# A reordering of the attention stages' queues in a macaron transformer block on one core

## The chip, the core and the metric

The kernel runs on one core of one Trainium2 chip. The metric is the device time of one execution in microseconds. All engines run side by side: TensorE (PE in the profile), VectorE (DVE), ScalarE (ACT), GpSimd (POOL) and the DMA queues of SyncE (SP); each executes its own list of instructions in the order in which it is written, and waits on semaphores that the others raise.

## The reference

The input x has 2 batches of 2048 rows of 256 numbers. Three blocks are added to it in turn, each of them reading a layer-normalised x:

```
x = x + 0.5 * ffn(layernorm(x))
x = x + attention(layernorm(x))
x = x + 0.5 * ffn(layernorm(x))

ffn:        gate = fp4(x) @ fp4(w_gate).T ; up = fp4(x) @ fp4(w_up).T
            h = silu(gate) * up           ; out = fp4(h) @ fp4(w_down).T
attention:  q, k, v = x @ W.T + b   (real and imaginary parts, 256 each)
            scores = (qr.kr + qi.ki) / 16 ; w = softmax(scores)
            out = stack(w @ vr, w @ vi) @ Wo + bo
```

`fp4` quantises blocks of 16 numbers to the FP4 grid and back. Everything is float32.

## The kernel before, in words

**Split numbers.** To keep float32 accuracy, a value that goes into TensorE is held as two float32r parts, the upper (`_hi`) and the lower (`_lo`), and a product is three matmuls.

**Attention.** The weights of queries and keys are multiplied together once, and so are those of values and output, so that attention has one key tensor `k`, one query tensor and one value tensor of width 256. The work goes in 8 stages, `n = 0 .. 7` (`NQ = 8`), each of 512 rows of queries; stages 0 to 3 belong to batch 0, stages 4 to 7 to batch 1 (`HQ = 4`). A stage walks over 16 chunks `c` of 128 keys (`CH = 16`). In this text S(n,c) is `scores(n, c)`, six matmuls of 512 columns, and W(n,c) is `weighted_values(n, c)`, twelve matmuls of 256 or 258 columns. For a chunk:

1. PE makes S(n,c) in one of two PSUM banks; `scores` waits until the copy out and the running maximum of chunk c-2 are done (`evac_done`, `top_done`).
2. ACT copies the scores to a ring in SBUF (`evacuate`, L1453); DVE keeps the running maximum (`running_top`, L913), which waits for that copy.
3. After the stage's last chunk, PE transposes the maximum, DVE reduces it and makes the shift, PE spreads the shift over a bank.
4. DVE subtracts the shift (`shifted`, L935), ACT takes the exponential (`exponential`, L1459) and writes the upper part (`p_upper`, L1469), POOL writes the lower part (`p_lower`, L553).
5. PE makes W(n,c), which waits for `p_lower`, and accumulates it in four banks. At the end of a stage DVE divides by the row sum and adds to x (`finish`, L939 and L945), after W(n,15).

Steps 4 and 5 of stage n-1 run beside steps 1 and 2 of stage n: on PE, S(n,c) and W(n-1,c') alternate. In most stages W(n-1,c-2) follows S(n,c). W(n-2,15) comes behind S(n,0). W(n-1,0) also waits for `finish(n-2)`. `p_upper(n,c)` waits for W(n,c-4), as there are four buffers of upper parts.

**Where the lists differ by stage.** At n = 3 and n = 7 `SCORES_ALONE` names chunks at which a score runs with no W behind it. At n = 1 and n = 5 the last two value tiles are made just ahead of the stage (`values_upper`, L1443, on ACT and `values_lower`, L898, on DVE). At n = 4 the batch changes: PE transposes the keys of batch 1 in groups (`transpose_keys(1, g)`, L1606, called TK1, TK2 and TK3 here for g = 1 to 3), ACT writes their upper part (`keys_upper`, L1244), DVE their lower part (`keys_lower`, L884), and `queries(4)` (L1908) is made from group 0. TK1 writes the banks in which the queries of stage 4 stand, so it waits until ACT's `queries_upper` (L1435) and DVE's `queries_lower` (L890) have read them (`qlo_done`). Its input `xn` is written by DVE or POOL (`keys_normalised`, L983 on DVE). TK2 waits for the lower part of group 1, TK3 for that of group 2, and S(4,0) for that of group 3.

**After attention.** The second FFN's first steps are laced into the last stage's W by an order written out by hand, and from there on a loop over 32 row tiles runs.

The order of all this is the order of the calls in each engine's block; no planner is involved.

Of the kernel before, what the change touches and what calls it, by code (L numbers as in the profile page):

```python
# [30 lines left out]
def macaron_kernel(nc, x_in, wq, bq, wk, bk, wv, bv, wo, bo, w_gate, w_up, w_down, out):  # L31
# [18 lines left out]
    NQ = NT // QT  # L50
    HQ = NQ // B
# [3 lines left out]
    LAST_ORDER = (2, 0, 1, 3)  # L55
    SCORES_ALONE = {HQ - 1: (7,), NQ - 1: (5, 9, 13)}
    PR = 4
# [9 lines left out]
    with ctx:  # L67
# [561 lines left out]
        def _(dve):  # L629
# [396 lines left out]
            for n in range(1, NQ):  # L1026
                if n == HQ:
# [3 lines left out]
                    for c in range(4):  # L1031
                        shifted(n - 1, c)
                    queries_lower(n, 0)
                    queries_lower(n, 1)
                    finish(n - 2)
                    shifted(n - 1, 4)
# [29 lines left out]
                if n % HQ == 1:  # L1066
                    values_lower(n // HQ, 6)
                shifted(n - 1, 0)
                shifted(n - 1, 1)
                if n % HQ == 1:  # L1070
                    values_lower(n // HQ, 7)
                if n >= 2 and n != HQ + 1:
# [53 lines left out]
        def _(act):  # L1126
# [371 lines left out]
            for n in range(1, NQ):  # L1498
                if n == HQ:
                    keys_upper(1, 0)  # L1500
                    for c in range(2):
                        exponential(n - 1, c)
                        p_upper(n - 1, c)
                    queries_upper(n)
                    for c in range(2, 4):
                        exponential(n - 1, c)
                        p_upper(n - 1, c)
                    exponential(n - 1, 4)
# [6 lines left out]
                    keys_upper(1, 2)  # L1515
                    exponential(n - 1, 7)
                    p_upper(n - 1, 7)
                    keys_upper(1, 3)
                    for c in range(8, 10):
                        exponential(n - 1, c)  # L1520
                        p_upper(n - 1, c)
                    for c in range(8):
                        if c + 10 < CH:
                            exponential(n - 1, c + 10)
                            p_upper(n - 1, c + 10)
                        evacuate(n, c)
# [13 lines left out]
                for c in range(CH):  # L1540
                    if n == NQ - 1 and c >= 9:
                        evacuate(n, c)
                        exponential(n - 1, c)
                        if c != 13 and c < CH - 1:
                            p_upper(n - 1, c if c < 13 else c - 1)
                    else:
                        exponential(n - 1, c)
                        p_upper(n - 1, c)
                        evacuate(n, c)
# [4 lines left out]
            n = NQ - 1  # L1554
            p_upper(n - 1, CH - 2)
            normalise(0)
            p_upper(n - 1, CH - 1)
            exponential(n, 0)
# [45 lines left out]
        def _(pe):  # L1604
# [413 lines left out]
            spread_shift(0)  # L2018
            values(0, 7)
            for n in range(1, NQ):  # L2020
                if n == HQ:
# [21 lines left out]
                    continue  # L2043
                alone = SCORES_ALONE.get(n, ())
                summed = 0
                for c in range(CH):
                    scores(n, c)
                    if c == 0 and n % HQ != 1:
                        weighted_values(n - 2, CH - 1)
                    if 2 <= c < CH - 1 and c not in alone:  # L2050
                        weighted_values(n - 1, summed)
                        summed += 1
                if n == HQ - 1:
# [4 lines left out]
                    spread_shift(n)  # L2058
                    weighted_values(n - 1, CH - 2)
                    queries(n + 1)  # L2060
                    weighted_values(n - 1, CH - 1)
                elif n + 1 < NQ:
# [74 lines left out]
```

## Time and profile before

| | us |
|---|---|
| three runs | 942.09, 942.96, 943.01 (median 942.96) |
| the profiled execution's own time | 942.09 |
| its span, first to last instruction | 940.3 |
| PE busy | 908.0 (97%) |
| DVE busy | 707.4 (75%) |
| ACT busy | 652.2 (69%) |
| POOL busy | 498.0 (53%) |
| attention, from the first query product to the last weighted value | about 279 to 719 |

In a line of the timeline the columns are: start and length in us, engine, line of the kernel, operation, tiles written and read, their shapes, a count where neighbours are merged, and in brackets the engine's idle time just before and what ended it. A length includes the way through the engine's pipeline, so two matmuls behind each other overlap: a 512-column matmul is listed with 0.39 us and the next starts 0.23 us later.

### The profile page before, as it was taken

The numbers are of one execution on the slowest core, as the hardware profiler recorded it, in microseconds if no ns is written. First come the engines' busy times: TensorE is split into PE (matmuls) and PEld (weight loads), VectorE is DVE, ScalarE is ACT, GpSimd is POOL, SyncE is SP. The second block draws the span as 40 slices with busy tenths as digits, with TensorE's granted clock in tenths as the row PEclk, the third lists the DMA queues.
The fourth block names the chain that finished last, engine by engine and source line by source line (L and its number), as shares of the span: only waits on it lengthen the run. The fifth ranks groups of instructions, "written<-read, shape, count | busy, mean of one in ns | idle before, by whom it ended". The sixth has DMA issues, their size and how long they took to land.

```text
span 940.3 us, 16317 instructions
## 1 busy us (share of the span) xinstructions
PE 908.0 (97%) x5704; PEld 811.5 (86%) x5704; DVE 707.4 (75%) x1163; ACT 652.2 (69%) x1368; POOL 498.0 (53%) x557
## 2 busy tenths in 40 slices
PE   3899999999999999999999999999998999999997
PEld 2778888888988799989998899998998988989887
DVE  7988988898777666655574544545598899999997
ACT  6677788888885475767675576767783777656554
POOL 3555677666630064535663064546577656756562
PEclk9999999999999999999999999999999999999999
DMA  9100000000000000000000000000000000000001
GB/s 319 48 1 1 1 1 1 2 1 1 1 1 2 1 1 1 1 1 2 1 1 1 1 1 1 1 2 1 1 1 1 1 24 24 23 23 24 5 20 45
DMA packets 11553, 13.83 MB, mean 15 GB/s; under 512 B 848, under 2 KB 10576, under 8 KB 11472
## 3 DMA queue, kind: packets, MB, share of 16 engines
q1 hardware_dynamic: 11472, 12.79, 4.1%
q8 instruction: 46, 0.75, 0.3%
q14 instruction: 35, 0.29, 0.1%
HBM read 8.59 MB, written 4.19 MB: 14 GB/s over the span
## 4 chain that ended last, share of the span: by engine, by line
PE 82%; DVE 9%; issue 3%; POOL 3%; ACT 3%; DMA 0%; SPq 0%; DVEq 0%; ACTq 0%; POOLq 0%
PE bank L1707 21%; PE bank L1945 18%; PE bank L1610 6%; PE bank_b L1718 6%; PE bank_b L1725 4%; PE bank L1983 4%; PE bank L1987 4%; PE bank L1985 4%; PE bank L1908 2%; PE bank L1746 2%; PE bank_b L1987 1%; PE bank_b L1983 1%; PE bank_b L1985 1%; POOL p_lo L553 1%; PE bank L1926 1%
## 5 line engine op out<-in xcount | busy, mean ns | idle before, releaser
L553 POOL TENSOR_TENSOR p_lo<-s_ring,p_hi 128x512 fp32r<-128x512 f32 x128 | 168.4, 1320 | 219.8 <-ACT p_hi L1469 219.7
L515 POOL TENSOR_TENSOR zq<-grid,s_neg 128x256 f32<-128x256 f32 (+2 forms) x184 | 173.3, 966 | 42.1 <-DVE grid L752 39.8
L913 DVE TENSOR_TENSOR top<-bank,top 128x512 f32<-128x512 f32 x112 | 77.4, 691 | 125.8 <-ACT s_ring L1453 125.7
L1707 PE MATMUL bank<-w_hi,T_hi 128*128 128x512 f32 (+1 forms) x384 | 150.6, 392 | 3.4 <-DVE z L711 2.5
L1707 PE MATMUL bank<-w_hi,T_lo 128*128 128x512 f32 (+1 forms) x384 | 144.9, 377 | 0.0
L1707 PE MATMUL bank<-w_lo,T_hi 128*128 128x512 f32 (+1 forms) x384 | 144.4, 376 | 0.0
L1453 ACT ACTIVATE s_ring<-bank 128x512 f32<-128x512 f32 x128 | 75.9, 593 | 78.0 <-PE bank L1945 77.9
L1292 ACT ACTIVATE T_hi<-bank 128x1024 fp32r<-128x1024 f32 (+1 forms) x68 | 64.6, 950 | 83.8 <-PE bank L1610 83.8
L1983 PE MATMUL bank<-v_hl,p_hi 128*128 128x258 f32 x384 | 109.9, 286 | 0.5 <-DVE x L945 0.3
L1987 PE MATMUL bank<-v_hl,p_lo 128*128 128x258 f32 x384 | 108.2, 282 | 0.0
L1985 PE MATMUL bank<-v_hl,p_hi 128*128 128x256 f32 x384 | 108.2, 282 | 0.0
L1945 PE MATMUL bank<-q_hi,k_hi 128*128 128x512 f32 x256 | 101.2, 395 | 0.8
L1945 PE MATMUL bank<-q_lo,k_hi 128*128 128x512 f32 x256 | 100.6, 393 | 0.0
L1945 PE MATMUL bank<-q_hi,k_lo 128*128 128x512 f32 x256 | 100.3, 392 | 0.0
L1459 ACT ACTIVATE s_ring<-s_ring 128x512 f32<-128x512 f32 x128 | 79.2, 622 | 18.6 <-DVE s_ring L935 18.6
L722 DVE TENSOR_REDUCE amax<-z 128x60 f32<-128x960 f32 (+2 forms) x72 | 74.9, 1040 | 17.4 <-ACT z L1326 14.5
L935 DVE TENSOR_TENSOR s_ring<-s_ring,bank 128x512 f32<-128x512 f32 x128 | 84.8, 677 | 1.3 <-PE bank L1610 0.9
L1469 ACT ACTIVATE p_hi<-s_ring 128x512 fp32r<-128x512 f32 x128 | 80.6, 632 | 6.4 <-PE bank_b L1987 2.8
L1707 PEld LDWEIGHTS bank<-w_hi,T_hi 128*128 128x128 f32 x384 | 72.9, 190 | 13.5 <-issue 3.6
L492 POOL TENSOR_TENSOR x<-x,down 128x256 f32<-128x256 f32 x62 | 46.9, 756 | 68.7 <-ACT down L1281 68.7
L1707 PEld LDWEIGHTS bank<-w_hi,T_lo 128*128 128x128 f32 x384 | 72.7, 189 | 11.0
L1707 PEld LDWEIGHTS bank<-w_lo,T_hi 128*128 128x128 f32 x384 | 73.1, 190 | 8.8
(223 smaller groups left out, 2288.5 us busy)
## 6 DMA issues: line engine op xcount, KB each, us to landing
out<-x SPq DMA_DIRECT2D x7, 512.0 KB, 2.9
x<-in_L_attn_hidden_states SPq DMA_DIRECT2D x3, 1024.0 KB, 14.3
x<-in_L_attn_hidden_states SPq DMA_DIRECT2D x2, 512.0 KB, 7.4
wraw<-in_L_ffn_w_down SPq DMA_DIRECT2D x1, 704.0 KB, 8.2
wraw<-in_L_ffn_w_gate SPq DMA_DIRECT2D x1, 640.0 KB, 4.4
wraw<-in_L_ffn_w_up SPq DMA_DIRECT2D x1, 640.0 KB, 6.1
wq_s<-in_L_attn_Wq SPq DMA_DIRECT2D x1, 512.0 KB, 8.2
wk_s<-in_L_attn_Wk SPq DMA_DIRECT2D x1, 512.0 KB, 9.2
```

Of the source, the lines that this page charges most:

```text
L515: last = nc.gpsimd.tensor_tensor(out=blocks(zq[:, to:to + hi - lo]), in0=blocks(grid[:, lo:hi]), in1=spread(s_neg[:, par, lo // BLOCK:hi / ...
L553: nc.gpsimd.tensor_tensor(out=lower_buf(n, c), in0=score_buf(n, c), in1=upper_buf(n, c).bitcast(F32), op=ALU.subtract).then_inc(plo_done, 1)
L913: nc.vector.tensor_tensor(out=top[:], in0=score_bank(c), in1=other, op=ALU.max).then_inc(top_done, 1)
L935: nc.vector.tensor_tensor(out=p, in0=p, in1=shift_bank, op=ALU.subtract).then_inc(diff_done, 1)
L1453: nc.scalar.activation(score_buf(n, c), score_bank(c), ACT.Copy).then_inc(evac_done, 1)
L1459: nc.scalar.activation(p, p, ACT.Exp, scale=SCALE).then_inc(exp_done, 1)
L1469: nc.scalar.activation(upper_buf(n, c), score_buf(n, c), ACT.Copy).then_inc(phi_done, 1)
L1707: last = nc.tensor.matmul(gu[:, lo:hi], lhsT=T[:, par, HK + kd, :], rhs=w[:, kd, lo:hi], start=n == 0, stop=n == len(terms) - 1)
L1945: last = nc.tensor.matmul(score_bank(c), lhsT=kk[:, kd, t], rhs=q[:, kd, :], start=i == 0, stop=i == len(terms) - 1)
L1983: nc.tensor.matmul(o[:, 0:D + 2], lhsT=hi[:, q], rhs=v_hl[:, c, 0:D + 2], start=c == 0, stop=False, skip_group_check=True)
L1985: nc.tensor.matmul(o[:, 0:D], lhsT=hi[:, q], rhs=v_hl[:, c, D + 2:], start=False, stop=False, skip_group_check=True)
L1987: last = nc.tensor.matmul(o[:, 0:D + 2], lhsT=lo[:, q], rhs=v_hl[:, c, 0:D + 2], start=False, stop=c == CH - 1, skip_group_check=True)
```

## The change

Nothing is computed differently; instructions change places in the lists of DVE, ACT and PE.

- PE, stages 3 and 7: `SCORES_ALONE` goes. W(n-1,0) follows S(3,3) at n = 3 and S(7,5) at n = 7, and from there every score has its W behind it.
- PE, end of stage 3: W(2,15) moves ahead of `queries(4)`.
- DVE, stage 4: `finish(2)` moves ahead of both `queries_lower`. Stages 1 and 5: `values_lower(., 7)` moves ahead of `shifted(., 0)` and `shifted(., 1)`.
- ACT, stage 4: chunks 2 and 3 (exponential and upper part) go ahead of `queries_upper(4)`; chunks 8 and 9 go ahead of `keys_upper(1, 3)`.
- ACT, stages 1 and 5: for chunks 0 to 2 the copy out of the new score goes ahead of the exponential and the upper part of the old one. Stage 7: exponential and upper part lag two chunks behind the copy out.
- ACT, behind stage 7: `normalise(0)` goes ahead of what is left of chunks 14 and 15.

```diff
-    SCORES_ALONE = {HQ - 1: (7,), NQ - 1: (5, 9, 13)}
 # DVE, n == HQ
                     for c in range(4):
                         shifted(n - 1, c)
+                    finish(n - 2)
                     queries_lower(n, 0)
                     queries_lower(n, 1)
-                    finish(n - 2)
 # DVE, other stages
                 if n % HQ == 1:
                     values_lower(n // HQ, 6)
+                    values_lower(n // HQ, 7)
                 shifted(n - 1, 0)
                 shifted(n - 1, 1)
-                if n % HQ == 1:
-                    values_lower(n // HQ, 7)
 # ACT, n == HQ
-                    for c in range(2):
+                    for c in range(4):
                         exponential(n - 1, c)
                         p_upper(n - 1, c)
                     queries_upper(n)
-                    for c in range(2, 4):
-                        exponential(n - 1, c)
-                        p_upper(n - 1, c)
...
                     keys_upper(1, 2)
-                    exponential(n - 1, 7)
-                    p_upper(n - 1, 7)
-                    keys_upper(1, 3)
-                    for c in range(8, 10):
+                    for c in range(7, 10):
                         exponential(n - 1, c)
                         p_upper(n - 1, c)
+                    keys_upper(1, 3)
 # ACT, other stages
                 for c in range(CH):
-                    if n == NQ - 1 and c >= 9:
+                    if n == NQ - 1:
+                        if c == 0:
+                            exponential(n - 1, 0)
+                        if c >= 4:
+                            exponential(n - 1, c - 2)
+                            p_upper(n - 1, c - 2)
+                        evacuate(n, c)
+                        if c == 1:
+                            p_upper(n - 1, 0)
+                        if c == 2:
+                            exponential(n - 1, 1)
+                        if c == 3:
+                            p_upper(n - 1, 1)
+                    elif n % HQ == 1 and c < 3:
                         evacuate(n, c)
                         exponential(n - 1, c)
-                        if c != 13 and c < CH - 1:
-                            p_upper(n - 1, c if c < 13 else c - 1)
+                        p_upper(n - 1, c)
                     else:
...
             n = NQ - 1
-            p_upper(n - 1, CH - 2)
             normalise(0)
-            p_upper(n - 1, CH - 1)
+            for c in (CH - 2, CH - 1):
+                exponential(n - 1, c)
+                p_upper(n - 1, c)
 # PE
-                alone = SCORES_ALONE.get(n, ())
-                summed = 0
+                lag = {HQ - 1: 3, NQ - 1: 5}.get(n, 2)
                 for c in range(CH):
                     scores(n, c)
                     if c == 0 and n % HQ != 1:
                         weighted_values(n - 2, CH - 1)
-                    if 2 <= c < CH - 1 and c not in alone:
-                        weighted_values(n - 1, summed)
-                        summed += 1
+                    if lag <= c < CH - 1:
+                        weighted_values(n - 1, c - lag)
...
                     weighted_values(n - 1, CH - 2)
+                    weighted_values(n - 1, CH - 1)
                     queries(n + 1)
-                    weighted_values(n - 1, CH - 1)
```

## Rows read from the trace of the kernel before

**Rows 1.** Windows: stretch, its length, then busy time of PE, PEld, DVE, ACT, POOL; PEclk.
```profile
325.40:372.75 47.35, 47.35 (x298) 42.61 (x297) 31.57 (x55) 32.64 (x64) 25.04 (x23) 1.00 0.00 1
...
464.04:488.60 24.56, 23.58 (x186) 22.55 (x185) 21.06 (x37) 16.16 (x25) 15.02 (x17) 1.00 0.00 1
...
633.69:673.11 39.42, 39.42 (x243) 35.18 (x241) 20.62 (x38) 30.70 (x70) 22.14 (x21) 1.00 0.01 1
673.11:723.40 50.29, 46.78 (x333) 43.59 (x332) 43.71 (x79) 31.77 (x60) 37.24 (x32) 1.00 0.00 1
```

**Rows 2.** Timeline, start of stage 1: DVE, ACT, POOL, PE.
```profile
325.00 1.27 DVE L935 TENSOR_TENSOR s_ring<-s_ring,bank 128x512 f32<-128x512 f32 x2
326.23 0.69 DVE L898 TENSOR_TENSOR v_hl<-bank_b,v_hl 128x512 fp32r<-128x512 f32 x1
...
326.10 0.62 ACT L1459 ACTIVATE s_ring<-s_ring 128x512 f32<-128x512 f32 x1
326.75 0.63 ACT L1469 ACTIVATE p_hi<-s_ring 128x512 fp32r<-128x512 f32 x1
327.29 0.58 ACT L1453 ACTIVATE s_ring<-bank 128x512 f32<-128x512 f32 x1
...
327.53 1.29 POOL L553 TENSOR_TENSOR p_lo<-s_ring,p_hi 128x512 fp32r<-128x512 f32 x1 [41.05 <-ACT p_hi L1469]
...
329.56 0.28 PE L1983 MATMUL bank<-v_hl,p_hi 128*128 128x258 f32 x1
```

**Rows 3.** Timeline, start of stage 3: PE, ACT, DVE.
```profile
421.69 0.39 PE L1945 MATMUL bank<-q_hi,k_hi 128*128 128x512 f32 x1
...
425.90 0.39 PE L1945 MATMUL bank<-q_hi,k_hi 128*128 128x512 f32 x1
...
427.27 0.28 PE L1983 MATMUL bank<-v_hl,p_hi 128*128 128x258 f32 x1
...
423.28 0.60 ACT L1453 ACTIVATE s_ring<-bank 128x512 f32<-128x512 f32 x1 [0.81 <-PE bank L1945]
...
424.71 0.23 DVE L939 RECIPROCAL rinv<-bank 128x1 f32<-128x1 f32 x2 [2.97 <-PE bank_b L1987]
...
427.21 0.68 DVE L913 TENSOR_TENSOR top<-bank,s_ring 128x512 f32<-128x512 f32 x1
```

**Rows 4.** Timeline, change of batch, stages 3 to 4: ACT.
```profile
468.52 0.63 ACT L1459 ACTIVATE s_ring<-s_ring 128x512 f32<-128x512 f32 x1 [1.89 <-DVE s_ring L935]
...
470.90 1.50 ACT L1435 ACTIVATE q_hi<-bank,bqk 128x512 fp32r<-128x512 f32 x2
...
485.96 1.03 ACT L1244 ACTIVATE k_hi<-bank 128x1024 fp32r<-128x1024 f32 x1 [2.17 <-PE bank L1606]
```

**Rows 5.** Timeline, change of batch: DVE.
```profile
471.60 1.58 DVE L890 SCALAR_TENSOR_TENSOR q_lo<-bank,bqk,q_hi 128x512 fp32r<-128x512 f32 x2 [1.33 <-ACT q_hi L1435]
...
475.66 1.67 DVE L983 TENSOR_SCALAR xn<-x,nmean,rstd 128x256 f32<-128x256 f32 x4
...
480.28 3.36 DVE L983 TENSOR_SCALAR xn<-x,nmean,rstd 128x256 f32<-128x256 f32 x4
...
487.02 1.22 DVE L884 TENSOR_TENSOR k_lo<-bank,k_hi 128x1024 fp32r<-128x1024 f32 x1 [0.46 <-ACT k_hi L1244]
```

**Rows 6.** Timeline, change of batch: PE, the three key transposes.
```profile
473.29 1.06 PE L1606 MATMUL bank<-ident,xn 128*128 128x128 f32 x8 [0.17 <-issue]
...
478.63 1.10 PE L1606 MATMUL bank<-ident,xn 128*128 128x128 f32 x8
...
484.83 1.09 PE L1606 MATMUL bank<-ident,xn 128*128 128x128 f32 x8 [0.81 <-DVE k_lo L884]
```

**Rows 7.** Timeline, behind stage 7: DVE, PE.
```profile
675.34 0.41 DVE L722 TENSOR_REDUCE amax<-z 128x16 f32<-128x256 f32 x1
...
723.40 1.62 PE L1610 MATMUL bank<-ident,zq 128*128 128x128 f32 x8 [2.62 <-DVE x L973]
```

**Rows 8.** Windows, columns as in Rows 1: PE's clock behind that wait.
```profile
723.40:727.54 4.14, 4.14 (x15) 3.59 (x16) 3.04 (x8) 1.05 (x2) 2.48 (x4) 0.59 0.00 0
```

More of the change, by code:

```diff
@@ L2019, in _ @@
             values(0, 7)
+            lag = 2
             for n in range(1, NQ):
```

## The prediction

> **What bounds the kernel now.** I read the windows by stage first, because the change touches single stages and a share over the whole span says nothing about them. Four stages get a new order on PE or ahead of it, 1, 3, 5 and 7; the first and the last of them stand in [rows 1]. PE is busy for 47.35 of 47.35 us in the one and for 39.42 of 39.42 us in the other. Nothing can be won inside these: no wait is there to be removed, and every wait that a new order makes is paid in full, since PE has no idle time to pay from. Idle time is found in two stretches only, 0.98 us in the change of batch (24.56 less 23.58) and 3.5 us behind stage 7 (50.29 less 46.78) [rows 1]. Then I read the timelines of all engines at the places where the lists change, and asked of each PE instruction how long before it its last input is ready. Where that slack is smaller than the delay that the change puts on the input, PE waits.
>
> **Stages 1 and 5.** Before, ACT does exponential(0,0) at 326.10, the upper part at 326.75 and the copy out of S(1,0) at 327.29; POOL's lower part runs 327.53 to 328.82, and PE takes W(0,0) at 329.56 [rows 2]. So the slack is 0.74 us. After, the copy out goes first, and it has to wait for S(1,0), which began only at 325.40, where the window starts. In stage 3 the copy out starts 1.59 us after its score does (423.28 against 421.69) [rows 3], so it starts here at 326.99. The exponential follows 0.54 us later, at 327.53, the upper part 0.65 us behind it (both steps as in [rows 2]), ending at 328.83, the lower part 0.15 us later for 1.29 us, until 330.3. W(0,0) can start at 330.35: 0.8 us late. The moved `values_lower(0, 7)` adds nothing to it: it cannot start before 326.23, and shifted(0,0) behind it ends at 326.23 + 0.61 + 0.68 = 327.5, just when ACT wants it. Before, shifted(0,0) ran at 325.00 and was covered; that cover is gone, but the copy out hides it. Stage 5 has the same list: 0.8 us again. For each I keep 0 (the slack is larger than it looks) and 1.2 us (both delays add up in part) as ends.
>
> **Stage 3.** S(3,3) now comes directly behind S(3,2). It needs the running maximum of chunk 1. DVE cannot make that before `finish(1)`, which itself waits for W(1,15), behind S(3,0): DVE starts it at 424.71 after 2.97 us of idle, and the maximum of chunk 1 ends at 427.21 + 0.68 = 427.89 [rows 3]. S(3,2) starts at 425.90 and PE is free at 427.27. Before, W(2,0) stood there and hid the maximum; now PE waits until about 427.95: 0.7 us. The lone score at chunk 7 that goes away had cost nothing, as PE was gapless. Bounds 0.4 and 1.0.
>
> **Stage 7.** The same at S(7,3), 0.7 us, with `finish(5)` in the place of `finish(1)`. Then S(7,4) and S(7,5) follow with nothing between, on two banks. S(7,5) needs S(7,3) (1.37 us), the copy out of it (0.2 us later, 0.60 us) and the maximum (0.69 us, and 0.1 us of handing over), 2.97 us in all [rows 3], where two scores take 2.75: 0.2 us more. Together 0.9 us, bounds 0.5 and 1.6. From S(7,6) on a W stands behind every score, ACT has 2.8 us for 1.8 us of work per chunk plus 1.4 us of statistics at every third, and the lag of two chunks leaves the inputs of W ready early: nothing there.
>
> **Change of batch, PE.** W(2,15) ahead of `queries(4)` costs PE nothing, and `finish(2)` can then run when DVE stands idle for 1.33 us [rows 5]. But this is not what TK1 waits for. It waits for `queries_lower(4, 1)`, and that hangs on ACT.
>
> **Change of batch, ACT.** The first exponential is at 468.52, `queries_upper` at 470.90, two chunks later [rows 4], so a chunk takes 1.19 us. With four chunks ahead, `queries_upper` starts at 473.28. TK1 started 2.39 us after it (473.29) [rows 6]; it will start at 475.67, 2.4 us later than before, while PE has the same work as before and stands idle for about 2.7 us. TK2 is bound by PE's own work and keeps its distance of 5.34 us [rows 6]: 481.0. `keys_normalised(3)` on DVE, which started at 480.28 and not on a wait [rows 5], must now wait until TK2 has read its input, 1.1 us after 481.0. Its four instructions take 3.36 us, where the four of `keys_normalised(2)` took 1.67 us [rows 5]; the slow ones ran beside POOL's lower parts, and those of chunks 5 and 6 fall there again. So they end at 485.5, the lower keys of group 2 (1.22 us) at 486.7, and TK3 starts then: 1.9 us late, since its old wait of 0.81 us has been used up. Shifted(3,8) follows on DVE, then the chunks 8 and 9 on ACT (2.4 us), which now stand ahead of `keys_upper(1, 3)`: it starts at 489.65 and not 1.13 us behind TK3 as before (485.96 against 484.83) [rows 4, 6]. With 1.03 us for it and 1.22 us for the lower part [rows 4, 5], S(4,0) can start at 492.0. Before it started at 488.60, the end of the window: 3.4 us. If `keys_normalised(3)` takes 1.67 us, the same sum gives 490.4, so 1.8 us is the lower end; 5.1 us is the upper one, with the clock (below).
>
> The SBUF page of the Trainium skill (section "Who interferes with whom") says that a tensor_scalar of VectorE in its two-port mode and an instruction of GpSimd take one pair of ports as a whole, and that the second to come stands until the first is done. The trace agrees: 0.42 us each without POOL beside it, 0.84 us on average with it. By that rule alone, with two lower parts of 1.29 us to stand for, the stall would be 2.6 us in place of 1.7 and the total 0.9 us more.
>
> **Behind stage 7.** `normalise(0)` comes about 1.5 us earlier on ACT. What reads it on DVE, at 675.34, shows no idle time before it [rows 7], so it was never late: nothing. The upper parts of chunks 14 and 15 still wait for W(6,10) and W(6,11).
>
> **The sum.** 0.8 + 0.8 + 0.7 + 0.9 + 3.4 = 6.6 us. Behind each of the five places PE, DVE and ACT hang on each other as before, so nothing gives it back. The profiled execution took 942.09 us (span 940.3 and 1.8 around it), which gives 948.7. It is the lowest of the three runs, 0.87 us under their median of 942.96, and I forecast on the median: 949.6 us.
>
> **The rivals.**
> Half clock: PE idle for 2.62 us at 723.40 [rows 7] was followed by 4.14 us at a mean granted clock of 0.59 [rows 8], between the levels of 2.4 and 1.2 GHz, which costs 4.14 x 0.41 = 1.7 us. The idle time of 2.7 us before TK1 is as long. For it: that row. Against it: it is a single case, and PE is dense up to that point here. TK2 and all behind it move by as much: 951.2 us.
> Hidden: the slacks are larger than I read them, or the handing over is shorter, and less than 1.9 us is left: about 943. It would take that the queue of ACT at the batch change does not bind, against [rows 4].
> Starved stage 7: the lag of two makes ACT's copies out late at every chunk, by 0.3 us at eleven of them, 3.3 us more: 952.9. Against it: the slack per chunk above.
> The other side: behind stage 7 the DVE chain up to the 2.62 us wait starts with the first quantised tile. If it hung on `normalise(0)`, its 1.5 us would come off that wait and the 1.7 us of half clock behind it would go too: 3.2 us. It decides from the point at which the five waits together are under 1.3 us; then the time is 939.8 us. Against it stands the missing idle time at 675.34. With my five waits in full the same would give 946.4.
> That the change doesn't do what it says can be left out: the lists are followed in order.
>
> **How the numbers follow.** Five waits at full clock 0.53 (own range 947.9 to 950.6, as the batch change gives 1.8 to 3.4 us or a little more), half clock 0.28, starved stage 0.09, hidden 0.06, the other side 0.04. A measurement of this kernel tells about 0.2% from no change, 1.9 us. So faster 0.04, same 0.05, slower 0.91, as the hidden case reaches a little beyond 1.9 us. The range goes from 945.8 (a few of the small waits hidden, or the tail's gain against all five) to 952.2 (half clock with 1 us more): outside it are the other side, the hidden case and the starved stage, 0.19.
>
> **What would show it.** PE idle of 0.8 us before the first L1983 of stages 1 and 5, released by POOL `p_lo`; 0.7 us before the fourth score of stages 3 and 7, released by DVE `top`; over 2 us before the first L1606 of the change of batch, released by DVE `q_lo`; about 1.5 us before S(4,0), released by DVE `k_lo`. Stages 2 and 6 keep their length. The clock right behind TK1 tells the first rival. I am wrong if stages 1, 3, 5 and 7 stay gapless, or if the stretch behind stage 7 gets shorter.

## The result, and the profile after

The changed kernel takes 950.21 us (median of 4 runs, 950.04 to 951.87), the kernel before beside it 942.99 us (4 runs, 942.09 to 943.60): a ratio of 1.0082 with a 95% interval of 1.0067 to 1.0096. It is slower, by 7.2 us; 949.6 was forecast. The profiled execution took 947.15 us, with a span of 945.4 us at a mean granted clock of 0.998; that of before took 942.09 us, 940.3 us at 0.996. So the profiles stand 5.1 us apart where the medians stand 7.2 apart. Between them lies the clock, as is shown below.

Windows of the changed kernel, stage by stage, each from its first score on PE to that of the next; columns as in Rows 1:
```profile
325.61:373.83 48.22, 47.56 (x298) 42.53 (x297) 33.15 (x55) 32.74 (x64) 24.95 (x23) 1.00 0.01 1
373.83:422.76 48.93, 48.93 (x310) 44.05 (x309) 30.46 (x63) 34.17 (x75) 23.80 (x20) 1.00 0.00 1
422.76:465.98 43.22, 42.61 (x266) 37.97 (x264) 20.66 (x38) 32.23 (x72) 24.59 (x24) 1.00 0.01 1
465.98:493.06 27.08, 23.42 (x185) 22.39 (x185) 19.90 (x37) 18.10 (x28) 17.33 (x19) 1.00 0.00 1
542.17:590.34 48.17, 47.62 (x298) 42.55 (x297) 24.26 (x39) 35.07 (x76) 24.67 (x23) 1.00 0.00 1
639.09:679.76 40.67, 39.90 (x242) 35.03 (x240) 20.54 (x38) 30.34 (x70) 22.08 (x21) 1.00 0.00 1
679.76:730.05 50.29, 46.80 (x333) 43.60 (x332) 43.86 (x79) 32.03 (x61) 37.27 (x32) 1.00 0.00 1
730.05:734.19 4.14, 4.14 (x26) 3.77 (x27) 3.54 (x9) 2.61 (x5) 2.97 (x4) 1.00 0.00 0
```
Beside [rows 1]: stage 1 was 47.35 us and is 48.22, the change of batch was 24.56 and is 27.08, stage 7 was 39.42 and is 40.67, and the 50.29 us behind it are the same to the hundredth. Stage 3 went from 42.35 to 43.22 and stage 5 from 47.31 to 48.17, while stage 2 (48.94 before) and stages 4 and 6 (49.03 and 48.75 before, 49.11 and 48.75 after) kept their lengths. The differences are 0.87, 0.87, 2.52, 0.86 and 1.25 us, 6.4 in all. The wait behind stage 7 ends 6.65 us later than before (730.05 against 723.40); the last 0.2 us is a later start of stage 1 (325.61 against 325.40), ahead of which no list is changed. The last line answers to [rows 8]: after the same wait the clock was 0.59 before and is 1.00 here. At that clock the stretch cost before 4.14 x 0.41 = 1.7 us more than here: this is why a program that comes 6.65 us late to the wait has a span only 5.1 us longer. It is no work of the change: of eleven traces with this wait the clock falls behind it in eight and stays in three, as is told in the last section.

The list of PE's waits of the changed kernel (total us, times, longest us):
```profile
PE bank L1616 <- DVE x L972: 2.6, 1, 2.6
PE bank L1612 <- issue: 2.3, 1, 2.3
...
PE bank L1989 <- POOL p_lo L552: 1.4, 3, 0.7
...
PE bank L1951 <- DVE k_lo L883: 1.3, 1, 1.3
PE bank L1951 <- DVE top L912: 1.2, 2, 0.6
```
The first was there before [rows 7], and so was one of the three L1989, with 0.2 us. The others are new, and they are the waits that were named: L1612 is the first transpose of keys, L1989 the first W of stages 1 and 5, L1951 the scores S(4,0), S(3,3) and S(7,3). The list names no engine for L1612; DVE's second `queries_lower` ends at 477.33, 0.1 us ahead of it. The old 0.8 us in front of the third transpose [rows 6] has left the list.

PE's timeline at these waits (start, length, in brackets the idle time before):
```profile
330.53 0.39 PE L1989 MATMUL bank<-v_hl,p_hi 128*128 128x258 f32 x1 [0.66 <-POOL p_lo L552]
...
429.12 0.47 PE L1951 MATMUL bank<-q_hi,k_hi 128*128 128x512 f32 x1 [0.61 <-DVE top L912]
...
477.43 1.06 PE L1612 MATMUL bank<-ident,xn 128*128 128x128 f32 x8 [2.35 <-issue]
...
487.85 1.04 PE L1612 MATMUL bank<-ident,xn 128*128 128x128 f32 x8
...
493.06 0.47 PE L1951 MATMUL bank<-q_hi,k_hi 128*128 128x512 f32 x1 [1.31 <-DVE k_lo L883]
...
645.43 0.47 PE L1951 MATMUL bank<-q_hi,k_hi 128*128 128x512 f32 x1 [0.63 <-DVE top L912]
```
A wait costs about 0.2 us more than the idle time in the brackets. Without a wait the next matmul starts 0.23 us behind the start of a 512-column one; with a wait the one ahead first runs out its listed 0.39 us, 0.16 us more. And the first matmul behind it is 0.47 us long in place of 0.39 (0.39 in place of 0.28 at L1989). Both stand in the busy time of the window. So the 0.66 us of idle in stage 1 and the 0.61 us at S(3,3) stand for 0.87 us of length each.

### The profile page after: what moved, and what is told of

Read it like the earlier page. It is cut to its first block, busy times and chain, and to the rows that moved or that the text cites. A ratio compares the mean times of both kernels' runs of the same rounds, so it can differ in the third digit from the quotient of the medians.

```text
span 945.4 us, 16317 instructions
## 1 busy us (share of the span) xinstructions
PE 908.1 (96%) x5704; PEld 810.2 (86%) x5704; DVE 708.8 (75%) x1163; ACT 652.2 (69%) x1368; POOL 496.9 (53%) x557
## 4 chain that ended last, share of the span: by engine, by line
PE 81%; DVE 9%; issue 3%; ACT 3%; POOL 3%; DMA 0%; SPq 0%; DVEq 0%; ACTq 0%; POOLq 0%
PE bank L1713 22%; PE bank L1951 17%; PE bank L1616 6%; PE bank_b L1724 6%; PE bank L1989 4%; PE bank_b L1731 4%; PE bank L1993 4%; PE bank L1991 4%; PE bank L1914 2%; PE bank L1752 2%; POOL p_lo L552 2%; PE bank_b L1993 1%; PE bank_b L1989 1%; PE bank_b L1991 1%; PE bank L1932 1%
## 5 line engine op out<-in xcount | busy, mean ns | idle before, releaser
L1989 PE MATMUL bank<-v_hl,p_hi 128*128 128x258 f32 x384 | 110.2, 287 | 1.7 <-POOL p_lo L552 1.4
L1951 PE MATMUL bank<-q_hi,k_hi 128*128 128x512 f32 x256 | 101.6, 397 | 3.5 <-DVE k_lo L883 1.3
L1951 PE MATMUL bank<-q_lo,k_hi 128*128 128x512 f32 x256 | 100.5, 393 | 0.0
L1951 PE MATMUL bank<-q_hi,k_lo 128*128 128x512 f32 x256 | 100.3, 392 | 0.0
L1724 PE MATMUL bank_b<-wd_hl,T_hi 128*128 128x256 f32 x600 | 80.3, 279 | 0.0
```

Source lines behind the costliest of these rows:

```text
L1724: nc.tensor.matmul(dn, lhsT=T_hi[:, par, k, :], rhs=wd_hl[:, k, half:half + D], start=n == 0, stop=False)
L1951: last = nc.tensor.matmul(score_bank(c), lhsT=kk[:, kd, t], rhs=q[:, kd, :], start=i == 0, stop=i == len(terms) - 1)
L1989: nc.tensor.matmul(o[:, 0:D + 2], lhsT=hi[:, q], rhs=v_hl[:, c, 0:D + 2], start=c == 0, stop=False, skip_group_check=True)
```

## The experiments

A profiled execution or a median can hold a stretch or two at half clock more or less. So each run is also given as its span times its mean granted clock, which is its length at full clock, as a difference from the kernel before (937.04 us in that measure; 937.01 to 937.19 in the several sets). The clock is listed to three digits, so this is good to about 0.5 us at best. The changed kernel, which ran beside several of these (25 runs, median 950.11), stands at +6.3 us with a mean clock of 0.9941; the kernel before has 0.9957.

The traces give a second and sharper measure, the length from the start of one stage's first score to that of the next, in us:

| run | stage 1 | stage 5 | stage 3 and change of batch | stage 7 to the end of the wait behind it |
|---|---|---|---|---|
| before | 47.35 | 47.31 | 66.91 | 89.71 |
| after | 48.22 | 48.17 | 70.30 | 90.96 |
| e1 | 47.32 | 47.35 | 70.59 (clock fell) | 89.67 |
| e2 | 47.31 | 47.35 | 67.78 | 90.91 |
| e3 | 48.23 | 48.18 | 66.93 | 89.71 |
| e4 | 47.32 | 47.35 | 71.09 (clock fell) | 89.67 |
| e5 | 47.32 | 47.30 | 68.52 | 89.73 |
| e6 | 48.21 | 48.17 | 68.85 | 91.04 |
| e9 | 47.32 | 47.32 | 68.29 | 89.64 |
| e11 | 48.15 | 48.08 | 66.91 | 89.71 |
| e12 | 48.74 | 48.74 | 66.94 | 89.72 |

A stretch that an edit leaves alone repeats within 0.1 us from trace to trace. The part of the program ahead of stage 0, which no edit touches, does not: the first score comes between 289.80 and 292.75 us. That is where much of the scatter of whole runs lies.

**The parts of the change, one by one.** First the batch change alone:
```diff
+                    finish(n - 2)                  # DVE, ahead of queries_lower
-                    for c in range(2):             # ACT, ahead of queries_upper
+                    for c in range(4):
-                    exponential(n - 1, 7); p_upper(n - 1, 7); keys_upper(1, 3)
-                    for c in range(8, 10): ...
+                    for c in range(7, 10): ...     # ACT, ahead of keys_upper(1, 3)
+                    weighted_values(n - 1, CH - 1) # PE, ahead of queries
```


> The kernel before with the change-of-batch part alone: on PE W(2,15) ahead of queries(4), on DVE finish(2) ahead of queries_lower, on ACT four chunks ahead of queries_upper(4) and chunks 8 and 9 ahead of keys_upper(1,3). Theory A (each place pays its own wait, and nothing gives it back): the stretch from the first transpose of the maximum to S(4,0) is 27.1 us as in the changed kernel, in place of 24.6, so about +2.5 us, ratio 1.0027; stages 1, 3, 5 and 7 stay gapless. Theory B (the idle time before TK1 also brings the half clock): in part of the executions 1.7 us more and a mean clock lower by 0.002 each time, so a median of +3.5 us or more and a wider spread than the kernel before. Theory C (the parts help one another in the changed kernel, so that the sum holds by chance): less than 1 us here.

945.70 us (6 runs), ratio 1.003 (1.0018 to 1.0041), +2.3 us at equal clock, mean clock 0.9950. In its trace the stretch up to S(4,0) is 3.68 us longer than before, with the clock fallen behind TK1 (0.58 over 4.00 us, which takes 1.7 us of clock); at full clock the changed kernel loses 2.52 us there. So the fall made this stretch 1.2 us longer and not 1.7: the wait of S(4,0) behind it is 0.92 us in e1 and 1.31 in the changed kernel. The measure at equal clock takes off the whole 1.7 and so reads a little low where this fall is in an execution.

Then the distances of stages 3 and 7, with ACT's list of stage 7 and `normalise(0)`:
```diff
-    SCORES_ALONE = {HQ - 1: (7,), NQ - 1: (5, 9, 13)}
+                lag = {HQ - 1: 3, NQ - 1: 5}.get(n, 2)
-                    if 2 <= c < CH - 1 and c not in alone:
+                    if lag <= c < CH - 1:
```


> The kernel before with the lags of stages 3 and 7 alone (the PE order of both, ACT's order in stage 7 and normalise(0) ahead of chunks 14 and 15). Theory A: 0.7 to 0.9 us before S(3,3), 0.8 us before S(7,3) and 0.3 us before S(7,5), all three released by DVE's running maximum: +2.0 us, ratio 1.0021. Theory C: the wait in stage 3 is taken back by the 0.81 us for which TK3 waited before, so +1.1 us only.

945.39 us (11 runs), 1.0016 (1.0007 to 1.0025), +2.8 us at equal clock, mean clock 0.9965. The table gives 0.87 + 1.20 = 2.07 us for the two stages, as was expected; by that the measure at equal clock is 0.7 us off here. How much of stage 7 is ACT's new order and not PE's was not run apart.

Then the start of stages 1 and 5:
```diff
+                    values_lower(n // HQ, 7)       # DVE, ahead of shifted(n - 1, 0)
+                    elif n % HQ == 1 and c < 3:    # ACT: the copy out first
+                        evacuate(n, c); exponential(n - 1, c); p_upper(n - 1, c)
```


> The kernel before with the orders of stages 1 and 5 alone (ACT copies out first for chunks 0 to 2, DVE does values_lower(.,7) ahead of shifted 0 and 1). Theory A: +0.87 and +0.86 us, 1.7 us together, ratio 1.0018, with PE waiting for POOL's first lower part in each. Rival: nothing measurable, since a batch change or the end of stage 7 has slack for a late PE: under 0.5 us.

943.57 us (11 runs), 1.0006 (0.9997 to 1.0015), +1.6 us at equal clock, mean clock 0.9965. By the ratio alone this part can't be told from nothing; by the measure at equal clock it is what two windows of 0.87 make. The lists of PE's waits of e2 and e3 hold the wait named for each:
```profile
PE bank L1953 <- DVE top L912: 1.2, 2, 0.6
```
```profile
PE bank L1986 <- POOL p_lo L553: 1.4, 3, 0.7
```
The three parts add up: 2.3 + 2.8 + 1.6 = 6.7 against 6.3 for the whole. The table says it more sharply: stages 1, 5 and 7 are lengthened by the same in e2 and e3 as in the changed kernel, within 0.1 us, and TK1 comes 53.8 us behind S(3,0) in e1 as it does in the changed kernel less the 0.87 us of stage 3. So there is no interplay between the stages.

**Inside the batch change.** Only chunks 2 and 3 ahead of the upper queries on ACT:
```diff
-                    for c in range(2):
+                    for c in range(4):
                         exponential(n - 1, c); p_upper(n - 1, c)
                     queries_upper(n)
```


> The kernel before with one edit: chunks 2 and 3 go ahead of queries_upper(4) on ACT. finish(2) stays behind queries_lower on DVE and W(2,15) behind queries(4) on PE. Theory A: TK1 waits some 2.4 us, TK3's old wait of 0.81 us shrinks, keys_upper(1,3) is not held up, S(4,0) comes 1.5 to 2 us later: ratio 1.0016 to 1.0021. Rival: the queue of ACT does not bind, the early finish(2) and W(2,15) make the loss in the changed kernel, and this one is within 0.3 us of the kernel before.

947.01 us (5 runs), 1.0038 (1.0025 to 1.0052), +2.1 us at equal clock, mean clock 0.9936. The ratio is above the expected one because the clock falls in these executions, as far as their mean clock and the trace tell. The wait and the window behind it:
```profile
PE bank L1603 <- issue: 2.8, 1, 2.8
```
```profile
476.66:481.00 4.34, 4.34 (x21) 4.34 (x22) 4.02 (x13) 1.54 (x2) 0.00 (x0) 0.50 0.00 0
```
The wait is 2.85 us where the changed kernel has 2.35. ACT shows why:
```profile
473.91 0.63 ACT L1469 ACTIVATE p_hi<-s_ring 128x512 fp32r<-128x512 f32 x1 [0.51 <-PE bank_b L1984]
```
This is the upper part of chunk 3, whose buffer comes free with W(2,15), and here W(2,15) still stands behind `queries(4)` on PE. So ACT's edit needs PE's: with W(2,15) ahead of the queries, as in e1, ACT does not wait there.

Only chunks 8 and 9 ahead of `keys_upper(1, 3)`:
```diff
                     keys_upper(1, 2)
-                    exponential(n - 1, 7); p_upper(n - 1, 7); keys_upper(1, 3)
-                    for c in range(8, 10): ...
+                    for c in range(7, 10): ...
+                    keys_upper(1, 3)
```


> The kernel before with one edit: chunks 8 and 9 go ahead of keys_upper(1,3) on ACT. Theory A: TK1, TK2 and TK3 start as before, keys_upper(1,3) starts some 2 us later and S(4,0) waits about 1.6 us for the lower keys, released by DVE: +1.6 us at equal clock. With the 2.2 us of the edit of queries_upper this would make 3.8 us if the two added up; the whole part measured 2.5, so they must overlap. Rival: ACT is not late here, since the exponential of chunk 8 waits for DVE anyway, and the cost is under 0.5 us.

944.39 us (11 runs), 1.001 (0.9999 to 1.002), +1.8 us at equal clock, mean clock 0.9964. S(4,0) waits 1.4 us, and the old wait in front of the third transpose stays:
```profile
PE bank L1943 <- DVE k_lo L884: 1.4, 1, 1.4
```
```profile
487.02 1.09 PE L1604 MATMUL bank<-ident,xn 128*128 128x128 f32 x8 [0.82 <-DVE k_lo L884]
```
Each of the two ACT edits costs by itself most of what both cost together (2.1 and 1.8 against 2.3 for the whole part; the table has 1.61 for e5, the 1.6 that was expected). They stand one behind the other: what the first makes late, the second need not wait for again.

The changed kernel with both ACT edits of the batch change undone:
```diff
-                    for c in range(4):
+                    for c in range(2):
                         exponential(n - 1, c); p_upper(n - 1, c)
                     queries_upper(n)
+                    ...                            # and keys_upper(1, 3) ahead of 8, 9
```


> The changed kernel with both ACT edits of the change of batch undone (queries_upper(4) behind two chunks again, keys_upper(1,3) ahead of chunks 8 and 9); DVE's early finish(2) and PE's early W(2,15) stay. Theory A: the loss of the change of batch lies in ACT's queue alone. But finish(2) now runs before queries_lower is possible, ends 2.0 us after W(2,15) and so holds queries_lower up by about 0.8 us: TK1 waits 0.7 to 0.9 us, the stretch to S(4,0) is 24.6 to 25.4 us against 27.1, the time 2 us lower than the changed kernel at equal clock. Rival: the PE and DVE moves carry the loss, and it stays within 0.5 us of the changed kernel.

947.33 us (5 runs), 1.0045 (1.0033 to 1.0058), +4.7 us at equal clock, mean clock 0.9964. This is more than the other stages make (3.85 us by the windows), and only 1.6 us less than the changed kernel, where 2 us had been expected. PE still waits 1.6 us for the first transpose, twice the expected 0.7 to 0.9:
```profile
PE bank L1617 <- issue: 1.6, 1, 1.6
```
ACT and DVE there:
```profile
475.40 0.69 ACT L1433 ACTIVATE q_hi<-bank,bqk 128x512 fp32r<-128x512 f32 x1 [0.65 <-PE bank L1919]
...
476.12 0.75 DVE L889 SCALAR_TENSOR_TENSOR q_lo<-bank,bqk,q_hi 128x512 fp32r<-128x512 f32 x1 [0.59 <-ACT q_hi L1433]
```
ACT now stands idle ahead of the upper queries and waits for PE: `queries(4)` come last on PE, and the way from them over ACT and DVE to TK1 has nothing on PE to lie beside. So PE's own edit, alone on the kernel before:
```diff
-                    queries(n + 1)
                     weighted_values(n - 1, CH - 1)
+                    queries(n + 1)
```


> The kernel before with one edit: on PE W(2,15) goes ahead of queries(4). My prediction put this move at nothing. New theory, from the run in which ACT's edits were undone and TK1 still waited 1.6 us: W(2,15) behind queries(4) was the cover for the way of the queries through ACT and DVE, and with it gone TK1 waits about 1.6 us here too, released by DVE's queries_lower; the time at equal clock rises by 1.0 to 1.5 us. The old step says: no wait of TK1 beyond the 0.2 us of the kernel before, no change.

943.88 us (12 runs), 1.001 (1.0 to 1.002), +1.2 us at equal clock against the runs of before in its own set (937.19 us), mean clock 0.9961; by the table +1.38 us. PE's timeline at the first and the third transpose:
```profile
474.77 0.95 PE L1606 MATMUL bank<-ident,xn 128*128 128x128 f32 x7 [1.61 <-issue]
...
486.27 1.09 PE L1606 MATMUL bank<-ident,xn 128*128 128x128 f32 x8 [0.82 <-DVE k_lo L884]
```
Against 0.17 and 0.81 us before [rows 6] that is 1.45 us more idle. It also settles what was expected of DVE's early `finish(2)`, that it holds TK1 up by 0.7 to 0.9 us: e6 has this move and e9 has not, and both wait the same 1.61 us for TK1, with the stretch up to S(4,0) 0.3 us shorter in e6 (68.85 less the 0.87 of stage 3, against 68.29).

**The two edits of stages 1 and 5, apart** (one run each). ACT's alone:
```diff
+                    elif n % HQ == 1 and c < 3:
+                        evacuate(n, c); exponential(n - 1, c); p_upper(n - 1, c)
```


> The kernel before with ACT's edit of stages 1 and 5 alone (copy out ahead of exponential and upper part for chunks 0 to 2). The prediction has this as the whole of the two waits: PE waits 0.55 to 0.66 us for the first lower part in each stage, as in the changed kernel. Rival: it takes both edits, and the wait is under 0.3 us here.

945.10 us, clock 0.996; one run says nothing of a difference in time this small, but its stages 1 and 5 are 0.80 and 0.77 us longer than before. Its list of waits has the POOL wait, 0.55 us in stage 1 and 0.49 in stage 5 (the list counts a third of 0.2 us, which the kernel before has too):
```profile
PE bank L1987 <- POOL p_lo L553: 1.2, 3, 0.6
```
DVE's alone:
```diff
                     values_lower(n // HQ, 6)
+                    values_lower(n // HQ, 7)
                 shifted(n - 1, 0)
                 shifted(n - 1, 1)
-                    values_lower(n // HQ, 7)
```


> The kernel before with DVE's edit of stages 1 and 5 alone (values_lower(.,7) ahead of shifted 0 and 1). The two delays run side by side, so this alone should make nearly the same wait: shifted(.,0) ends 1.8 us later and the first lower part with it, a PE wait of 0.5 to 0.7 us in each stage. Rival: DVE has time here, and PE stays gapless.

947.84 us, clock 0.993. Stages 1 and 5 are 1.39 and 1.43 us longer than before. PE waits 1.15 us in each of the two stages, more than with both edits together, and it waits for another thing, at a score and not at a W. PE and ACT there:
```profile
332.34 0.47 PE L1944 MATMUL bank<-q_hi,k_hi 128*128 128x512 f32 x1 [1.15 <-ACT s_ring L1452]
```
```profile
330.42 0.63 ACT L1458 ACTIVATE s_ring<-s_ring 128x512 f32<-128x512 f32 x1 [1.35 <-DVE s_ring L935]
...
331.62 0.58 ACT L1452 ACTIVATE s_ring<-bank 128x512 f32<-128x512 f32 x1
```
With ACT's old list the exponential heads the queue and stands 1.35 us for the late shift; the copy out of S(1,0) behind it comes too late to free the bank that S(1,2) needs. I had expected the lower part as the releaser, with 0.5 to 0.7 us; that was wrong.

**Behind stage 7.** The 2.62 us wait [rows 7] was untouched by the change, but it is the one idle time from stage 0 on behind which the clock of the kernel before falls. In the first of these the first of the four last tiles is finished ahead of the scales of the third quantised tile:
```diff
                 to_grid(1)
+                finish_last(0, 1)
                 scales(2, 0)
-                finish_last()
+                finish_last(1, QT)
```


> The kernel before with one edit behind stage 7: on DVE the first of the four last output tiles (the one whose bank the next transposes overwrite) is finished ahead of scales(2) and not behind it. In the kernel before PE waits 2.6 us there for exactly this. Clock theory (idle time of PE of over 2 us is what lets the clock fall to half there in part of the executions): the wait falls to about 0.3 us, and no execution shows the half clock in this place. If PE sets the time of what follows: -2.3 us, and up to 1.7 us more in the mean from the clock, ratio 0.9960 to 0.9975. Rival: DVE is the bound from there on (95% busy), its list is not shorter, and the time is within 1 us of the kernel before.

940.47 us (11 runs), 0.9977 (0.9968 to 0.9986), −1.2 us at equal clock, mean clock 0.9968. It beats both kernels, by less than the 2.3 us at full clock that were expected if PE set the time here: the wait went to 0.81 us and not to 0.3. PE's timeline and the window behind the wait:
```profile
723.23 1.09 PE L1613 MATMUL bank<-ident,zq 128*128 128x128 f32 x8 [0.81 <-DVE x L975]
```
```profile
723.23:727.40 4.17, 4.17 (x25) 3.62 (x26) 4.03 (x12) 2.63 (x5) 2.26 (x3) 1.00 0.00 0
```
All four tiles ahead of these scales:
```diff
+                finish_last(0, QT)
                 scales(2, 0)
-                finish_last()
```


> As the run before this one, but all four last tiles go ahead of scales(2) on DVE. They wait for the last W, some 1 us more than the first of them alone, and that delays scales(2) by it. Expected: the same gain or 0.5 us less. If DVE sets the time of what follows, this one is slower than the one before by the idle time that it brings DVE, up to 1 us.

940.69 us (11 runs), 0.998 (0.9971 to 0.9989), −1.0 us at equal clock: the same, and 0.79 us of the wait are left.

The first tile ahead of the grid of the second quantised tile as well:
```diff
+                finish_last(0, 1)
                 to_grid(1)
                 scales(2, 0)
```


> The kernel before with the first of the four last output tiles finished on DVE ahead of to_grid(1), one step earlier than in the run that was faster. The wait of 0.8 us that was left before PE's transposes goes too, and DVE loses about 0.6 us of idle time waiting for the last W of that tile. If PE is the bound: 0.5 to 0.8 us faster than that run. If DVE is the bound there: as fast as that run, or up to 0.6 us slower.

940.87 us (8 runs), 0.9974 (0.9963 to 0.9984), −0.9 us at equal clock (−1.1 against the runs of before in its own set), as fast as e7 and not faster. The wait for the transpose is gone, and another comes behind it:
```profile
727.38 1.41 PE L1721 MATMUL bank_b<-wd_hl,T_hi 128*128 128x256 f32 x10 [0.67 <-DVE x L975]
```
All three take 1.8 us or more off the one wait and give 1 us or so at equal clock; in e7 0.4 us comes back as a gap of PE in front of a later DVE result, in e10 the 0.67 us above. The rest of this stretch is DVE's, and taking a wait away at one place shows it at the next.

## Why the prediction was right, and where it was not

**Stages 1 and 5** (0.8 each; the windows grew by 0.87 and 0.86). Right in size and chain. ACT and POOL of the changed kernel:
```profile
327.19 0.60 ACT L1451 ACTIVATE s_ring<-bank 128x512 f32<-128x512 f32 x1 [0.78 <-PE bank L1951]
327.76 0.63 ACT L1457 ACTIVATE s_ring<-s_ring 128x512 f32<-128x512 f32 x1
328.43 0.63 ACT L1467 ACTIVATE p_hi<-s_ring 128x512 fp32r<-128x512 f32 x1
...
329.20 1.28 POOL L552 TENSOR_TENSOR p_lo<-s_ring,p_hi 128x512 fp32r<-128x512 f32 x1 [42.53 <-ACT p_hi L1467]
```
The copy out starts 1.58 us behind its score (325.61), where 1.59 was read from stage 3; the rest follows as in [rows 2]. But "the moved `values_lower(0, 7)` adds nothing" holds only beside ACT's edit. By itself DVE's edit makes waits of 1.15 us (e12), ACT's by itself 0.55 and 0.49 (e11), and both together 0.66 and 0.55, so beside ACT's edit DVE's adds 0.1 us a stage. The copy out that goes first is the cover of the later shift: the prediction said so ("the copy out hides it"), and e12 gives the price without it.

**Stage 3** (0.7; measured 0.87). Right: the maximum of chunk 1 runs from 428.28 to 428.97, and S(3,3) starts at 429.12, 0.15 us behind it where I took 0.06. With the longer first matmul that is the difference.

**Stage 7** (0.9; measured 1.25). The wait at S(7,3) is 0.63 us idle and 0.79 from start to start; S(7,5) starts 0.53 us behind the last matmul of S(7,4) in place of 0.23, so 0.30 where 0.2 was forecast, too little to leave idle time in the list; and two longer first matmuls of 0.08 each come on top: 1.25. The starved stage is refuted: from S(7,6) on no wait for a copy out stands in the list.

**The change of batch** (3.4; measured 2.52). The order of events was right, and one duration was not. With the stages ahead of it at +0.87, +0.87 and 0.21 us, everything forecast there has to be moved by 1.95 us. Then TK1 was due at 477.6 (it started at 477.43), `keys_normalised(3)` at 484.05 (483.83), and then:
```profile
483.12 2.59 POOL L552 TENSOR_TENSOR p_lo<-s_ring,p_hi 128x512 fp32r<-128x512 f32 x2 [1.09 <-ACT p_hi L1467]
```
```profile
483.83 2.68 DVE L982 TENSOR_SCALAR xn<-x,nmean,rstd 128x256 f32<-128x256 f32 x4 [0.92 <-PE bank L1612]
...
491.69 1.23 DVE L883 TENSOR_TENSOR k_lo<-bank,k_hi 128x1024 fp32r<-128x1024 f32 x1 [2.26 <-ACT k_hi L1242]
```
```profile
490.65 1.01 ACT L1242 ACTIVATE k_hi<-bank 128x1024 fp32r<-128x1024 f32 x1
```
`keys_normalised(3)`, the DVE line at 483.83, took 2.68 us and not 3.36, so it ended at 486.51, 0.9 us ahead of the forecast 487.4; TK3 (487.85 for 488.6), `keys_upper(1, 3)` (490.65 for 491.6) and S(4,0) (493.06 for 493.9) are early by the same 0.8 to 1.0. That is the whole of 3.4 − 2.5: 0.2 us of it come from the earlier TK1, and 0.7 from the mis-sized term, "Its four instructions take 3.36 us". I had carried the length over from before, but what keeps still is the end: POOL's two lower parts end at 485.71 here and DVE 0.80 us later, with two free instructions; before, POOL ended at 483.17 (480.58 + 2.59) and DVE at 483.64, 0.47 later, with one. DVE started 0.3 us ahead of POOL's pair then [rows 5] and 0.7 us behind its start now. One by one, the second and third of the four before, with POOL's pair, and below them the second of the changed kernel:
```profile
480.61 1.41 DVE L983 TENSOR_SCALAR xn<-x,nmean,rstd 128x256 f32<-128x256 f32 x1
...
481.94 1.37 DVE L983 TENSOR_SCALAR xn<-x,nmean,rstd 128x256 f32<-128x256 f32 x1
...
480.58 2.59 POOL L553 TENSOR_TENSOR p_lo<-s_ring,p_hi 128x512 fp32r<-128x512 f32 x2 [1.38 <-ACT p_hi L1469]
```
```profile
484.49 1.38 DVE L982 TENSOR_SCALAR xn<-x,nmean,rstd 128x256 f32<-128x256 f32 x1
```
And four of the changed kernel with no POOL beside them:
```profile
478.60 1.38 DVE L982 TENSOR_SCALAR xn<-x,nmean,rstd 128x256 f32<-128x256 f32 x4 [0.68 <-PE bank L1612]
```
Each of the slow ones ends about 0.15 us behind the end of a lower part (482.02 and 483.31 before, 485.87 here, against 481.87, 483.17 and 485.71). Four in the open take 1.38 us together; the 1.67 us of [rows 5], from which the prediction had its 0.42, are not free of POOL, since their first one ran beside the end of POOL's earlier pair. The rule from the Trainium skill that the prediction weighed (SBUF — State Buffer, "Who interferes with whom"), that the one that comes second stands until the first is done, agrees with these ends; the 0.84 us on average of the prediction is no rate, but two instructions of 0.4 us and two of 1.4. Taken as a sum of two lower parts to stand for, as it was there, it would have made the term larger (by 0.9 us), the wrong way.

**"W(2,15) ahead of `queries(4)` costs PE nothing"** failed. Alone it costs 1.2 us and leaves PE 1.6 us idle (e9), and it is why undoing the two ACT edits doesn't bring the batch change back (e6). In the changed kernel it doesn't show, since ACT's four chunks hold `queries_upper` back for longer still: TK1 comes 0.8 us later there than in e6, counted from S(3,0). Beside ACT's edit the move even gives 0.5 us back: without it, in e4, TK1 comes 2.67 us later than before, with it, in e1, 2.20. I had asked only what W(2,15) itself waits for, and not what PE had to do while ACT and DVE worked on the queries. The forecast of the total is right here in spite of that step, and the 2.2 us by which TK1 is late are not ACT's alone: PE's move by itself makes 1.4 of them.

**Behind stage 7** (0; measured 0.0). Right: 50.29 and 50.29 us. The other side is refuted.

**The sum** came closer than its terms. The change of batch was forecast 0.9 us too long, the other four places 0.65 us too short (0.07, 0.06, 0.17 and 0.35), and so 6.6 us stand against 6.37 in the windows. That they nearly cancel is luck, and so is it that the median of the runs, 7.2 us above that before, lies as near to 6.6 from the other side: what it has on top is clock, as far as the next paragraph can tell.

**Half clock behind TK1** (chance 0.28). The profiled execution of the changed kernel doesn't have it (the whole window is at 1.00). But the same wait of 2.4 us in e1 has, and the stretch of the batch change at 0.94:
```profile
475.79:479.79 4.00, 4.00 (x21) 4.00 (x22) 2.44 (x6) 1.66 (x2) 0.00 (x0) 0.58 0.00 0
...
464.34:492.59 28.25, 24.94 (x186) 23.92 (x185) 19.49 (x37) 18.28 (x28) 17.34 (x19) 0.94 0.00 1
```
The two kernels whose profiled execution has it there, e1 and e4, are the ones with the low mean clocks, 0.9950 and 0.9936, and the changed kernel has 0.9941. By that 0.0016 of 944 us, 1.5 us, is a slower clock in the mean, and the median at the clock that the runs had is +7.1 (950.11 less 943.06) where the one at equal clock is +6.3. So this rival was not instead of the five waits but on top of them, in a part of the executions. That the clock falls behind TK1 in the unprofiled runs of the changed kernel is argued from its mean, not shown. A mean does not say where the clock fell: it falls in every profiled execution between 25 and 61 us as well, ahead of all edits, and not equally often. Here are the windows of that part in the kernel before and in e8, whose execution had a mean of 0.995 with the clock at full behind TK1 and behind stage 7:
```profile
25.00:60.00 35.00, 31.27 (x158) 25.20 (x159) 32.93 (x63) 22.41 (x50) 15.69 (x22) 0.95 0.05 17
```
```profile
25.00:60.00 35.00, 31.66 (x147) 25.70 (x148) 30.80 (x62) 21.22 (x48) 14.97 (x21) 0.85 0.05 16
```

## What to carry to other kernels

Where an engine is gapless, ask of each reordering what work lies beside each chain over the other engines, and take the cover of two edits together: one may be free only because of the other, and a costly one may be masked by a costlier. Of an operation that contends with another engine carry the end relative to that engine's work over to the new place, not its length. When differences are under 0.3%, compare times at equal clock (span times granted clock), since the raw medians here mix up to a microsecond and a half of it in; and better still compare the lengths of single stages between traces, which repeated within 0.1 us where the measure at equal clock was up to 0.7 us off.

## What the hardware showed

The clock's fall behind an idle PE is a matter of the execution and not of the kernel alone. With the same wait of 2.62 to 2.64 us behind stage 7, the 4.14 us behind it ran at a mean clock of 0.59 to 0.67 in eight profiled executions (before, e1, e3, e4, e6, e9, e11, e12) and at full clock in three (after, e2, e5). Behind TK1 it fell after 2.39 us (e1) and 2.85 us (e4) of idle, not after 2.35 (after) nor after 1.61 (e6, e9). Behind the 0.81 and 0.79 us of e7 and e8 it did not fall. Each of the stretches shown behind a wait is 4.0 to 4.3 us at 0.50 to 0.59, and takes 1.7 to 2.2 us of clock; behind TK1 only 1.2 us of the 1.7 came through to the length (e1). The Trainium skill (TensorE: Matmul & The Clock Gate, section "What's actually happening") has the clock fall after PE has been idle, as in those eight; no run here shows what sets it apart in the executions that keep it. That is left open.
